# bfloat16 one-hots and weights in three parts in the pair-count stage of a graph network, and three score loads on another queue

## The reference

```python
h = jnp.einsum('nd,hdf->nhf', x, W)
e = leaky_relu(a_src[src] + a_dst[dst], 0.2)
ex = jnp.exp(e - segment_max(e, dst)[dst])
out = segment_sum(h[src] * (ex / segment_sum(ex, dst)[dst])[:, :, None], dst)
```

## Time and profile before

| | us |
|---|---|
| profiled execution, device time | 6352.34 |
| its span | 6349.1 |
| median of the three timed runs | 6361.24 |
| TensorE matmuls busy | 4763.1 (75%) |
| VectorE busy | 4615.4 (73%) |
| ScalarE busy | 2165.1 (34%) |
| GpSimd busy | 2965.5 (47%) |
| granted clock of TensorE, mean | 0.875 |

### The profile page before, as it was taken

The page is one execution under the profiler, slowest core; times in us unless marked ns, Lnnn a source line. Parts: engine busy times, 40 slices in busy tenths (PEclk is TensorE's granted clock), DMA queues, the critical chain, the costliest instruction groups (busy, mean ns, idle before and its releaser), DMA issues.

```text
span 6349.1 us, 81975 instructions
## 1 busy us (share of the span) xinstructions
PE 4763.1 (75%) x22785; PEld 3319.6 (52%) x22785; DVE 4615.4 (73%) x5602; ACT 2165.1 (34%) x3980; POOL 2965.5 (47%) x3112
## 2 busy tenths in 40 slices
PE   7826999994999633577774777777778999964548
PEld 4415888873888533233333656666666555451213
DVE  9796776444999699899996888888875000159796
ACT  5633343332555143455552222222205000133223
POOL 0077777777777777882002777777730000000000
PEclk9999999997999855799996887888788999957777
DMA  9993444445999799653224666666641444136573
GB/s 244 278 239 81 140 139 139 138 137 189 311 310 312 256 341 327 215 163 91 71 73 139 217 215 218 216 217 221 216 91 51 150 153 150 39 84 218 176 228 126
DMA packets 695980, 1161.89 MB, mean 183 GB/s; under 512 B 268058, under 2 KB 483589, under 8 KB 681702
## 3 DMA queue, kind: packets, MB, share of 16 engines
q1 hardware_dynamic: 327403, 534.89, 29.2%
q0 software_dynamic: 134656, 328.87, 16.7%
q10 hardware_dynamic: 233594, 293.96, 13.4%
HBM read 672.47 MB, written 484.93 MB: 182 GB/s over the span
## 4 chain that ended last, share of the span: by engine, by line
PE 31%; DVE 30%; POOL 18%; issue 11%; DMA 6%; SPq 1%; ACT 1%; ACTq 1%; DVEq 0%; POOLq 0%
POOL slots_by_block_pair L962 13%; PE psall L1553 10%; PE psall L1704 8%; DVE arena L2287 6%; DVE arena L2297 6%; DVE arena L2258 6%; DMA arena<-table_x,arena 5%; POOL arena L995 4%; PE psall L1637 4%; DVE arena L2351 3%; DVE arena L2514 3%; POOL idle L964 1%; PE psall L1411 1%; PE psall L1668 1%; PE psall L1476 1%
## 5 line engine op out<-in xcount | busy, mean ns | idle before, releaser
L995 POOL DMA_INDIRECT arena<-table_x,arena x856 | 956.2, 1117 | 825.7 <-DMA arena<-slots_by_src 548.3
L962 POOL DMA_INDIRECT slots_by_block_pair<-arena x806 | 827.8, 1027 | 573.6 <-DVE arena L2039 314.6
L1614 PE MATMUL psall<-arena 128*65 128x313 f32 (+1 forms) x2800 | 867.9, 453 | 263.7 <-DVE arena L2297 263.7
L984 POOL DMA_INDIRECT slots_by_src<-arena,pos_s x806 | 918.5, 1140 | 253.8 <-issue 231.9
L1637 PE MATMUL psall<-arena 128*125 128x256 f32 x1712 | 571.6, 506 | 354.4 <-DVE arena L2351 354.4
L1154 ACT ACTIVATE arena<-psall 128x500 f32<-128x500 f32 (+3 forms) x668 | 306.1, 465 | 1372.9 <-PE psall L1649 1047.9
L1614 PEld LDWEIGHTS psall<-arena 128*65 128x65 f32 (+1 forms) x2800 | 337.4, 130 | 793.2 <-DVE arena L2297 404.8
L1520 PE MATMUL psall<-shared_w,arena 128*128 128x256 f32 x3264 | 750.4, 383 | 1.4 <-DVE arena L2191 1.4
L1553 PE MATMUL psall<-arena 128*128 128x250 f32 x2880 | 626.2, 377 | 105.8 <-DVE arena L2238 79.5
L1637 PEld LDWEIGHTS psall<-arena 128*125 128x125 f32 x1712 | 434.3, 260 | 468.6 <-DVE arena L2351 374.4
L1520 PEld LDWEIGHTS psall<-shared_w,arena 128*128 128x128 f32 x3264 | 605.7, 191 | 75.9 <-DVE arena L2191 1.6
(11 more groups left out here) (331 smaller groups left out, 7037.0 us busy)
## 6 DMA issues: line engine op xcount, KB each, us to landing
arena<-slots_by_src SPq DMA_DIRECT2D x107, 1040.0 KB
filters<-arena ACTq DMA_DIRECT2D x204, 520.0 KB, 2.7
arena<-filters POOLq DMA_DIRECT2D x202, 520.0 KB, 5.9
slots_by_src<-shared_on SPq DMA_DIRECT2D x8, 9230.0 KB, 77.5
weights_out<-arena ACTq DMA_DIRECT2D x125, 320.0 KB, 3.1
arena<-counts SPq DMA_DIRECT2D x50, 781.5 KB, 4.3
counts<-arena ACTq DMA_DIRECT2D x125, 312.5 KB
weights_in<-arena ACTq DMA_DIRECT2D x125, 312.5 KB
```

Of the source, the lines that this page charges most:

```text
L962: G.indirect_dma_start(slots_c, bass.IndirectOffsetOnAxis(ap=pos_c[:, j, q:q + 1], axis=0), rec_c[:, c, :], None).then_inc(s["scattered_c" ...
L984: G.indirect_dma_start(slots_s, bass.IndirectOffsetOnAxis(ap=pos_s[:, c:c + 1], axis=0), ring_s[:, g % SLOTS, c % TG, :], None).then_inc(r ...
L995: G.indirect_dma_start(hg[:, f % 2, j, :], None, t_x1, bass.IndirectOffsetOnAxis(ap=pay_s[:, f % 2, j, S_IDX:S_IDX + 1].bitcast(I32), axis ...
L1614: last = MM(ps[gat_bank(n, wn, h_, c)][0:F + 1, 0:z - a], rows, g["e1"][:, q % g["RE"], a:z], start=(b == 0), stop=(b == NT - 1))
```

## The change

- **Types.** Row of numbers, one-hots and weights become bfloat16. The row and the one-hots hold whole numbers up to 127, which bfloat16 holds exactly. A weight becomes the sum of three bfloat16 numbers, `high`, `mid` and `low`, so that their products with 0 and 1, summed in fp32, give the fp32 weight back.
- **VectorE, once in 14 steps** (`run_records`, nine times): sources and destinations of 168 tiles are copied to bfloat16, each value twice side by side (`twice`); the weights are split and doubled in the same way, and copied to PSUM. These are eight operations, five of them with a wait for their own end.
- **VectorE, each step:** the same three operations. Operands are read in pairs: the row of numbers two columns at a time, against a value that stands there twice. The one-hots are 126 (EVEN) and 128 columns wide; the multiplication makes three weighted one-hots, 12 x 3 x 126 elements. One input of each still comes from PSUM.
- **TensorE, each tile:** three bfloat16 matmuls in place of one fp32: one of 250 columns (destination one-hot and `high`), and two of 125 (`mid`, `low`) onto the weights' columns. Each has the source one-hot as its stationary operand.
- **Loads of the scores:** SyncE, not ScalarE, loads heads 0 to 2, after all tiles (`cb_mm`), each with a semaphore of its own. VectorE takes the heads in the order 3, 0, 1, 2 and waits for each one's load only where it first needs it.

```diff
+            link(V.tensor_copy(row_2.bitcast(BF16), iota[:, :]))
+            link(V.tensor_copy(row_p, row_2))
+            def run_records(run):
+                t0, n = RUN_T * run, min(RUN_T, T1 - RUN_T * run)
+                of = pay_c[:, t0:t0 + n, :]
+                for c, at in ((0, C_S), (1, C_D)):
+                    V.tensor_copy(twice[:, run % 3, c, 0:n, :], of[:, :, at:at + 1].to_broadcast([LANES, n, 2]))
+                high, mid, low = (w_parts[:, c, 0:n, :] for c in range(3))
+                rest = w_rest[:, 0:n]
+                link(V.tensor_copy(high, of[:, :, C_W:C_W + 1].to_broadcast([LANES, n, 2])))
+                link(V.tensor_tensor(rest, of[:, :, C_W], high[:, :, 0], ALU.subtract))
+                link(V.tensor_copy(mid, rest.unsqueeze(2).to_broadcast([LANES, n, 2])))
+                link(V.tensor_tensor(low, rest.unsqueeze(2).to_broadcast([LANES, n, 2]), mid, ALU.subtract))
+                link(V.tensor_copy(run_weights(run), w_twice))
...
-                V.tensor_tensor(ohd, by_d, of_tiles(pay_c, C_D, at, P), ALU.is_equal)\
+                V.tensor_tensor(by_twos(ohd[sl]), row(EVEN), paired(1, EVEN), ALU.is_equal)\
                     .then_inc(s["cb_oh"], 1)
-                V.tensor_tensor(ohs[sl], by_s, of_tiles(pay_c, C_S, at, LANES), ALU.is_equal)\
+                V.tensor_tensor(by_twos(ohs[sl]), row(LANES), paired(0, LANES), ALU.is_equal)\
                     .then_inc(s["cb_oh"], 1)
                 turn_wait(dve, s["cb_oh"], 3, CT_R, it, sl, c=1)
-                weights = psall[:, weights_at(n):weights_at(n) + CT_G]
-                V.tensor_tensor(wdd, ohd, weights.unsqueeze(2).to_broadcast([LANES, CT_G, P]),
+                weights = run_weights(run).bitcast(BF16).rearrange("p (t u) -> p t u", u=2)[:, 3 * t0:3 * (t0 + CT_G)]
+                V.tensor_tensor(ohw[sl].rearrange("p j a (k u) -> p (j a) k u", u=2),
+                                ohd[sl].unsqueeze(2).to_broadcast([LANES, CT_G, 3, EVEN]),
+                                weights.unsqueeze(2).to_broadcast([LANES, 3 * CT_G, EVEN // 2, 2]),
                                 ALU.mult).then_inc(s["cb_oh"], 1)
...
-                        MM(psall[:, bass.ds(half_at(mine[k], j), 2 * P)], ohs[sl][:, TG * k + j, :],
-                           ohw[sl][:, TG * k + j, :, :].rearrange("p a k -> p (a k)"),
+                        at, by_s = half_at(mine[k], j), ohs[sl][:, TG * k + j, :]
+                        MM(psall[:, bass.ds(at, 2 * P)].rearrange("p (a k) -> p a k", a=2), by_s,
+                           count_and_weight(sl, TG * k + j),
+                           start=False, stop=False, skip_group_check=True)
+                        MM(psall[:, P:][:, bass.ds(at, P)], by_s, ohw[sl][:, TG * k + j, 1, 0:P],
+                           start=False, stop=False, skip_group_check=True)
+                        MM(psall[:, P:][:, bass.ds(at, P)], by_s, ohw[sl][:, TG * k + j, 2, 0:P],
                            start=False, stop=False, skip_group_check=True).then_inc(s["cb_mm"], 1)
...
+            sp.wait_ge(s["cb_mm"], 1 + T1)
+            for h in range(HEADS - 1):
+                sp.dma_start(by_block[:, h, :, 0:P], scores_of(h)).then_inc(as_head[h], 16)
...
-            for h in range(HEADS - 1):
-                act.dma_start(by_block[:, h, :, 0:P], scores_of(h)).then_inc(s["as_more"], 16)
```

More of the change, by code:

```diff
@@ L94 @@
 LASTS = NB // 4
+RUN_S = 512 // (3 * CT_G)
+RUN_T = RUN_S * CT_G
 assert 4 * LASTS + 1 == NB and T1 < 2048
@@ L269, in gnn_kernel, with count_and_weight @@
         tjunk = view(o_e + 4 * EP, LANES, NB)
-        o_ohw = o_diag + HALF
-        o_both = o_ohw + 4 * CT_G * P
+        o_parts_1 = o_diag + HALF
+        o_both = o_parts_1 + 4 * CT_G * EVEN
         stage_both = view(o_both, LANES, 2 * 3 * PAIRS * P).rearrange("p (a b k) -> p a b k", a=2, k=P)
         assert o_both + 2 * 3 * PAIRS * P <= o_rec
[L275 to L280, removed]
+        o_parts_3 = o_b + 2 * NT * EVEN
+        assert T1 * C_REC <= 2 * NT * EVEN and 2 * CT_G * EVEN <= NT * EVEN
+        ohs = [view(o_oh_b + n * CT_G * LANES // 2, LANES, CT_G * LANES // 2).bitcast(BF16)
+               .rearrange("p (j k) -> p j k", j=CT_G) for n in range(CT_R)]
+        o_ohd = (o_parts_1, o_parts_1 + 2 * CT_G * EVEN, o_parts_3)
+        ohd = [view(o_, LANES, CT_G * EVEN // 2).bitcast(BF16).rearrange("p (j k) -> p j k", j=CT_G) for o_ in o_ohd]
+        ohw = [view(o_ + CT_G * EVEN // 2, LANES, 3 * CT_G * EVEN // 2).bitcast(BF16)
+               .rearrange("p (j a k) -> p j a k", j=CT_G, a=3) for o_ in o_ohd]
+        def count_and_weight(sl, j):
+            first_, apart_ = 2 * o_ohd[sl] + EVEN * j, CT_G * EVEN + 2 * EVEN * j
+            return arena[0:LANES, :].bitcast(BF16)[:, first_:first_ + 2 * apart_]\
+                .rearrange("p (a k) -> p a k", a=2)[:, :, 0:P]
+        o_twice = o_oh_b + CT_R * CT_G * LANES // 2
+        twice = view(o_twice, LANES, 3 * 2 * RUN_T).bitcast(BF16).rearrange("p (r c t u) -> p r c t u", r=3, c=2, u=2)
+        w_twice = view(o_twice + 6 * RUN_T, LANES, 3 * RUN_T)
+        w_parts = w_twice.bitcast(BF16).rearrange("p (t c u) -> p c t u", c=3, u=2)
+        w_rest = view(o_twice + 9 * RUN_T, LANES, RUN_T)
+        row_2 = view(o_twice + 10 * RUN_T, LANES, LANES // 2)
+        assert o_twice + 10 * RUN_T + LANES // 2 <= o_tab
         ctd = view(o_cb, LANES, 2 * N).rearrange("p (r s d) -> p r s d", r=2, s=NT)
@@ L487, in gnn_kernel, with run_weights @@
         run_w = ps[7][:, LANES:512]
-        IN_RUN = 512 // CT_G
-        def weights_at(n):
-            return 512 * (4 + n // IN_RUN) + CT_G * (n % IN_RUN)
+        row_p = ps[7][:, 0:LANES // 2]
+        row_b = row_p.bitcast(BF16)
+        def run_weights(run):
+            return ps[4 + run % 3][:, 0:3 * RUN_T]
         s = {n: sem(n) for n in """zeroed r_dve r_pe cleared consts in_edges in_ew in_x filled blank_c blank_s w_small w_more w_next  ln_stats link   go pool_go
@@ L513, in gnn_kernel @@
         fst = [sem(f"filt_st{n}") for n in range(SLOTS)]
+        as_head = [sem(f"as_head{n}") for n in range(HEADS - 1)]
         NODE = dict(a=(0, 1, 2, 3, 5), t=(0, 2, 3, 5, 8, 9), c=(0, 2, 3, 5, 8, 9), m=(0, 3, 5, 6, 7, 8, 9),
@@ L2227, in pair_onehots, with paired @@
             def pair_onehots(n):
                 it, sl = divmod(n, CT_R)
-                ohd, wdd = ohw[sl][:, :, 0, :], ohw[sl][:, :, 1, :]
+                run, t0 = n // RUN_S, CT_G * (n % RUN_S)
+                if n % RUN_S == 0:
+                    run_records(run)
                 turn_wait(dve, s["cb_mm"], CT_G, CT_R, it, sl, back=CT_R, base_=1)
-                at = CT_G * n
-                V.tensor_tensor(ohd, by_d, of_tiles(pay_c, C_D, at, P), ALU.is_equal)\
+                def paired(c, width):
+                    return twice[:, run % 3, c, t0:t0 + CT_G, :].unsqueeze(2).to_broadcast([LANES, CT_G, width // 2, 2])
@@ L2233, in pair_onehots, with by_twos, row @@
+                def by_twos(ap):
+                    return ap.rearrange("p j (k u) -> p j k u", u=2)
+                def row(width):
+                    return row_b[:, 0:width].rearrange("p (k u) -> p k u", u=2).unsqueeze(1)\
+                        .to_broadcast([LANES, CT_G, width // 2, 2])
+                V.tensor_tensor(by_twos(ohd[sl]), row(EVEN), paired(1, EVEN), ALU.is_equal)\
                     .then_inc(s["cb_oh"], 1)
-                V.tensor_tensor(ohs[sl], by_s, of_tiles(pay_c, C_S, at, LANES), ALU.is_equal)\
+                V.tensor_tensor(by_twos(ohs[sl]), row(LANES), paired(0, LANES), ALU.is_equal)\
@@ L2241, in _ @@
                 pair_onehots(n)
-            dve.wait_ge(s["as_in"], 16)
-            dve.wait_ge(s["as_more"], 48)
+            dve.wait_ge(s["cb_mm"], 1 + T1)
             halves = psall.bitcast(BF16)
@@ L2254, in _ @@
                     cut = slice(EVEN * j0, EVEN * j1)
-                    for h_ in range(HEADS):
-                        if i or n or h_:
-                            dve.wait_ge(s["x_max"], HEADS * (2 * i + n) + h_)
+                    for k, h_ in enumerate((HEADS - 1, *range(HEADS - 1))):
+                        if i == 0 and n == 0:
+                            dve.wait_ge(s["as_in"] if k == 0 else as_head[h_], 16)
+                        if i or n or k:
+                            dve.wait_ge(s["x_max"], HEADS * (2 * i + n) + k)
                         V.tensor_tensor_reduce(mjunk[:, 0:EVEN * (j1 - j0)].rearrange("p (b k) -> p b k", k=each),
```

3 lines of the change are left out of this document (1 added, 2 removed).

## The result

| | median us | lowest to highest | profiled execution, span |
|---|---|---|---|
| before | 6360.58 | 6352.69 to 6371.05 (4) | 6352.3, 6349.1 |
| after | 6481.38 | 6464.02 to 6486.34 (4) | 6464.0, 6462.1 |

A forecast was written before the change was run, and what follows sets the result against it. VectorE was to pace the pair-count stage: 0.8 + 37 preparation + 500 operations + 4 + 15 = 557 us against 661. Execution 6352.3 - 104 - 6 for score loads = 6242, timed 6250 us; range 6200 to 6365.

The forecast's parts named there:

- TensorE's issue: Pair-count stage: issuing three matmuls a tile was taken at 0.33 us a tile, 4.0 us a step, 5.0 at worst.
- rival B: TensorE stays the stage's bound through weight loads, issue or a lower clock: 6300 to 6345, say 6320 us; 0.16 with C.
- twin stage: Stage used to scale issue: 12 tiles, two records of 125 columns each, take 3.37 us, 0.28 a tile.
- Rival A: VectorE does not pair elements with one input in PSUM: stage 1016 us, kernel 6710 us; chance 0.18.
- VectorE's operations: Stage's three two-tensor operations run at double rate: 0.94, 0.96 and 2.5 us, 4.17 us a step, 500 us in all.
- The preparation: VectorE's doubled copies and weight split, once in 14 steps: 4.1 us a run, 37 us for nine, bounds 25 and 50.
- The rest of the stage: The whole pair-count stage, counted from VectorE's first copy: 557 us against 661, 104 us less.
- the slip: Stage allowance for DMA and ScalarE, both close behind VectorE: 15 us added, 0 to 50.
- The clock: Part of B: TensorE's granted clock falls to the 1.2 GHz level while waiting for VectorE; 500 columns take 431 ns again.
- The score loads: After the stage, moving three loads from ScalarE to SyncE wins 6 us; ends 5 us lost and 25 us won.
- the early head: Before the maxima, VectorE starts on the head already there (first operation 2.26 us), part of the 6 us won.
- GpSimd's later cover: The earlier attention stage slows POOL's scatter sooner, but it is idle from 2900 on, so that costs nothing.

The follow-up runs named there:

- e2: The changed kernel without the third matmul of each tile (lowest bfloat16 part left out of the sums): 6465.94 us, ratio 1.0181.
- e3: The changed kernel with constant addresses for each tile's sums, no shift, mask or address instruction per tile: 6283.03 us in one run, ratio 0.9895.
- e1: The changed kernel with weighted one-hots laid ahead of the plain one, so a tile needs one address instruction, not two: 6321.65 us, ratio 0.9961.
- e7: The kernel of e5 with table words loaded 24 at a time every six steps, not 12 every three: 6285.28 us, ratio 0.9899.
- e5: The kernel of e1 with table fields one bit lower, so the first tile of four needs no shift: 6293.26 us, ratio 0.9919.
- e4: The kernel before with only the three score loads moved to SyncE and the heads taken 3, 0, 1, 2: 6349.97 us, ratio 1.0005.

## Why the prediction was wrong

**The step that failed is TensorE's issue.** The prediction took 0.33 us a tile, "between 0.22 and 0.42", and from the issue 5.0 us a step "at worst". It had the right candidate (rival B: "issue of six instructions a tile") and the wrong unit. It scaled the twin stage's 0.28 us a tile by the count of weight loads and matmuls, six over four. These cost next to nothing: a weight load follows the last at the same address by 15 ns, and leaving 1440 of them out saved 5 us (e2). What costs are the register instructions, 91 to 97 ns each, and the change raised their number from three to four a tile. The prediction counted one address for the old tile and three for the new (there are two), and put the shift, the mask, the waits' ALU_OPs and the table loads at nothing, although the trace of the kernel before has their rows (L1553 above). Counted so, a tile is 0.309 us and 0.12 to 0.13 for the second address, 0.44 in all. Then come two ALU_OPs for each wait and, every three steps, a table load of 1.2 us and more. Most of this fp32's 0.431 us of array time had covered, and the lighter matmuls no longer do. A step takes 6.57 us, 5.43 before. The measured time, 6481 us, lies outside the range (6200 to 6365). B's own figure, 6320, was 160 short, and A, which reached further, had another mechanism.

**VectorE's operations: right.** 947, 948 and 2508 ns; forecast 0.94, 0.96 and 2.5. With one operand in PSUM the rate of two elements at a time holds here: 4536 elements in 2.51 us are 0.55 ns each, where fp32 takes 1.04. The tier table of the Trainium skill's "VectorE: DVE Perf Modes", by which these would take 8.12 us a step, is contradicted by these rows; its "Vector Engine (DVE) Microarchitecture Reference", section 5.1, agrees with them. Rival A falls. (Of the two rows that gave the 1.04, the one of 400 elements writes fp16, not fp32 as the prediction says; its slope came out all the same.)

**The preparation: within its bounds (25 to 50 us), below the 37 taken.** A full run's casts and subtractions are 0.39 to 0.51 us each, the scattered ones 0.39 where 0.5 to 0.75 was taken, and the copy into PSUM 0.69. Nine runs are busy for 28 us and take 30 to the next one-hot.

**The rest of the stage: right in total.** With constant addresses the stage took 549 us from first to last matmul, as the forecast had it (557 us with the copies ahead). In part that is luck: the preparation was 7 us shorter than taken, and VectorE's wait for TensorE 11 us longer than the slip.

**The clock.** Rival B also named a granted clock that falls. It did (0.86 in the stage, 0.50 without the third matmul), and the fall to 0.50 did not lengthen the stage where issue sets the pace (783.8 us against 788.6).

**The score loads: 6 us forecast, none measured.** That lies within the bounds, 5 us lost to 25 won. VectorE did not start on the head already there: the maxima began 5 us after ScalarE's first widening of the counts, as before. What binds is the counts' arrival. The prediction named it and still took 6 us for the issue and the early head.

**GpSimd's later cover.** That GpSimd "is idle from 2900 on the earlier trace rows, so that costs nothing" was wrong in the one run at the forecast's own speed: with the stage at 549 us (e3) the scatters ended at 3316, and some 24 us of the gain went there. The slack was 509 us in the profile of the kernel before; the shorter stage took 104 of it, and one instruction 391.

## What to carry to other kernels

Count an engine's register instructions when operands are addressed by registers, take their cost from the distance between their start times and not from their lengths, and ask what pace they would set if the array's time, which covers them now, fell. Before an fp32 matmul is split into lighter ones, lay out the operands so that all parts of a tile start at the same address. When a stage is made faster, look at what ran beside it on GpSimd: slack that one execution shows can be gone in another.

## What the runs showed of the hardware

- TensorE's sequencer: register instructions recorded as 36 ns start 97 ns apart; a second register address costs 0.12 us a tile (167.5 us over 1440 tiles, e1); two weight loads with the same address start 15 ns apart (after). The distances between register instructions are the same at granted clock 1.00 (after, at 1700 us) and 0.50 (e2).
- A table load of 12 words stopped the sequencer for 1.2 us at the median (0.85 to 2.96), one of 24 words for 2.9 us on average (e7; 12 words in e5: 1.7).
- VectorE's two-tensor operations of bfloat16, with one input in PSUM and pairs innermost: 0.55 ns an element at 4536 elements.
- One indirect DMA on GpSimd lasted 391 us (e3) and 390 us (e4) beside the attention's VectorE operations; the median is 0.96 us, and up to 2.63 in the kernel before.
